# Moving two experts' up-products into the attention's last values, and what follows them one expert on

## The reference

```python
xn = layernorm(x)
s  = attn(xn)              # 16 heads of 8, window 128, softmax; + gated state-space branch; + MLP
g  = silu(ffn(xn))         # 8 experts, top 2, each 128 -> 2*128 -> 128
out = x + s * g

# in attn:
x1  = x + g*attn_out + (1-g)*ssm_out      # g = sigmoid(h @ Wg + bg)
h2  = layernorm(x1) * ln2_g + ln2_b       # the "second norm"
s   = x1 + gelu(h2 @ W1 + b1) @ W2 + b2
# in ffn, all experts for all rows, weighted by combine (0 where not chosen):
p1  = normed @ mlp1[e].T + bias           # "up-products": gate half and linear half
act = min(g, 7) * sigmoid(1.702*g) * (clip(lin, -7, 7) + 1)
out = xc + sum_e combine[e] * (act @ mlp2[e].T + bias)
```

## Time and profile before

| | us |
|---|---|
| runs of the kernel | 1091.38, 1097.93, 1089.91 |
| median | 1091.38 |
| profiled execution | 1094.57 |
| its span, first to last instruction | 1092.8 |
| mean granted TensorE clock | 0.925 of 2.4 GHz |

### The profile page before, as it was taken

One profiled execution on the slowest core, in us unless ns is written; L12 is line 12 of the kernel. 1 busy time (PEld: TensorE's weight loads), 2 busy tenths in 40 slices (PEclk: granted clock), 3 DMA queues, 4 the chain that ended last, 5 costly groups with the idle time before them and its releaser, 6 DMA issues.

```text
span 1092.8 us, 38402 instructions
## 1 busy us (share of the span) xinstructions
PE 919.2 (84%) x15864; PEld 561.7 (51%) x15864; DVE 782.5 (72%) x1990; ACT 712.8 (65%) x1126; POOL 501.8 (46%) x786
## 2 busy tenths in 40 slices
PE   2567898989889898988889898989888898978877
PEld 1333564646455464645555464645555464635435
DVE  4476777887877677888777777887777788656216
ACT  3205685858677595858768595867768585746645
POOL 6226355372736356273626456273635547152331
PEclk7557999999999899999999999998999999978869
DMA  5552414123332404224241503223241402310000
GB/s 108 129 118 67 93 46 105 32 94 64 100 62 75 90 27 108 50 90 62 92 75 53 112 24 109 52 90 63 75 93 36 111 17 99 58 31 6 25 1 10
DMA packets 85599, 75.24 MB, mean 69 GB/s; under 512 B 9329, under 2 KB 79154, under 8 KB 85426
## 3 DMA queue, kind: packets, MB, share of 16 engines
q1 hardware_dynamic: 83346, 72.00, 28.3%
q10 hardware_dynamic: 2080, 0.79, 0.3%
HBM read 36.33 MB, written 30.15 MB: 61 GB/s over the span
## 4 chain that ended last, share of the span: by engine, by line
PE 48%; DVE 25%; issue 13%; ACT 9%; POOL 2%; DMA 2%; DVEq 0%; SPq 0%; POOLq 0%; ACTq 0%
PE ps L558 8%; DVE mx L1074 6%; PE ps L500 6%; PE ps L690 5%; PE ps L750 5%; PE ps L711 5%; ACT pt L831 4%; PE ps L489 3%; DVE gc L1131 3%; PE ps L570 2%; DVE lin L1124 2%; PE ps L575 2%; ACT ot L836 2%; DVE junk L950 2%; PE ps L684 2%
## 5 line engine op out<-in xcount | busy, mean ns | idle before, releaser
L831 ACT ACTIVATE pt<-ps 128x1024 f32<-128x1024 f32 (+1 forms) x256 | 234.7, 917 | 212.5 <-PE ps L489 211.1
L1074 DVE TENSOR_REDUCE mx<-ps 128x2 f32<-128x320 f32 (+1 forms) x512 | 230.9, 466 | 110.6 <-PE ps L515 107.6
L1253 POOL TENSOR_SCALAR_AFFINE_SELECT pt<-pt 128x512 f32<-128x512 f32 x256 | 170.7, 669 | 264.6 <-ACT pt L831 264.3
L500 PE MATMUL ps<-kd,qz 48*32 48x160 bf16 (+1 forms) x4096 | 160.5, 241 | 66.6 <-DVE mx L1074 34.2
L489 PE MATMUL ps<-qz,kd 51*32 51x256 bf16 (+1 forms) x4096 | 183.5, 272 | 6.1 <-ACT pt L831 3.8
L558 PE MATMUL ps<-pt,va 128*32 128x256 f32 (+1 forms) x2048 | 159.8, 397 | 33.2 <-ACT ot L836 33.0
L500 PEld LDWEIGHTS ps<-kd,qz 48*32 48x32 bf16 x4096 | 72.7, 91 | 218.7 <-issue 121.3
L690 PEld LDWEIGHTS ps<-m,act_t 128*128 128x128 f32 x1024 | 126.8, 191 | 53.6 <-DVE act_t L1152 38.6
L690 PE MATMUL ps<-m,act_t 128*128 128x128 f32 x1024 | 143.2, 283 | 11.6 <-DVE act_t L1152 11.6
L1256 POOL TENSOR_SCALAR_AFFINE_SELECT pt<-pt 128x512 f32<-128x512 f32 x192 | 124.6, 649 | 0.0
L879 ACT ACTIVATE lin<-ps,mbias 128x512 f32<-128x512 f32 x128 | 87.7, 685 | 48.7 <-DVE act_t L1152 29.5
(11 more groups left out here) (158 smaller groups left out, 1672.7 us busy)
## 6 DMA issues: line engine op xcount, KB each, us to landing
qz<-qk_parts SPq DMA_DIRECT2D x32, 384.0 KB, 7.3
kd<-qk_parts SPq DMA_DIRECT2D x32, 384.0 KB, 8.7
qk_parts<-qp SPq DMA_DIRECT2D x16, 384.0 KB, 2.4
qk_parts<-kp SPq DMA_DIRECT2D x16, 384.0 KB, 2.3
xl<-L_attn_x SPq DMA_DIRECT2D x16, 256.0 KB, 3.1
qk_parts<-qp SPq DMA_DIRECT2D x16, 256.0 KB, 2.9
qk_parts<-kp SPq DMA_DIRECT2D x16, 256.0 KB, 2.7
xnr<-xn SPq DMA_DIRECT2D x16, 256.0 KB, 3.3
```

The source lines that it names most:

```text
L500: nc.tensor.matmul(ps[QG * c:QG * (c + 1), 4 + par, w * pr:w * (pr + 1)], qz[q][rows, 2 * g + pr, P * i + QG * c:P * i + QG * (c + 1)], kd ...
L831: nc.scalar.activation(to, src, ACT.Exp, scale=SCALE).then_inc(exp_ok.sem, 1)
L1074: nc.vector.tensor_reduce(mx[:, i, HG * g + pr:HG * (g + 1):2], src, AX.X, ALU.max).then_inc(mx_ok.sem, 1)
L1253: sel1 = nc.gpsimd.affine_select(out=pt[:, s, :, 0:P], in_=pt[:, s, :, 0:P], compare_op=ALU.is_ge, fill=0.0, base=0, pattern=[[0, HG], [1, ...
```

## The change

up(0) and the broadcast for expert 0 (now share(0), with a signal share_ps of its own) go behind values 13 (n = 16) on TensorE. up(1) and the transposes of nm go behind values 14 (n = 17). share(1) goes behind the transposes of ao, ahead of the product with wo, and waits for nmT, which leaves its bank 5. ScalarE no longer waits for the broadcast: up_ps stands for the two halves alone, and VectorE's gate waits for share_ps. ScalarE does lin(0) and ga(0) first and then aoT and nmT, ahead of lin(1). On VectorE both steps of the residual, the statistics of x1 and their moments come one expert later, and the first half of norm_stats comes behind expert 0 instead of 2. h2 goes from behind expert 4 to behind expert 5 (AT_H2), its transposes on TensorE from behind down(4) to behind share(7), ahead of down(5), and norm_x from behind expert 7 to behind expert 6, where it stands ahead of the copy to h2T.

```diff
-AT_H2 = 4
+AT_H2 = 5
...
+        share_ps = signal("share_ps", E)
...
+                def up(e):
+                    k = 3 * (e % 2)
+                    if e == 0:
+                        pe.wait_ge(*done(nfT_ok, b))
+                        pe.wait_ge(*done(exp_ok, b))
+                    elif e == 1:
+                        pe.wait_ge(*done(s1_ok, b))
+                        if nx2:
+                            pe.wait_ge(*done(gpre_ok, b + 2))
+                        if nxt:
+                            pe.wait_ge(*done(cT_ok, b + 1))
+                            pe.wait_ge(*done(mx_ok, b + 1))
+                    else:
+                        pe.wait_ge(*done(ga_ok, b, e - 1))
+                    for s in range(2):
+                        mm = nc.tensor.matmul(bank(k + s), m1[:, e, s], nfT[:, q], start=True, stop=True)
+                    mm.then_inc(up_ps.sem, 1)
+
+                def share(e):
+                    if e >= 2:
+                        pe.wait_ge(*done(gc_ok, b, e - 1))
+                    elif e == 1 and nxt:
+                        pe.wait_ge(*done(nmT_ok, b + 1))
+                    nc.tensor.matmul(bank(3 * (e % 2) + 2), sel[:, e], cT[:, q], start=True, stop=True).then_inc(share_ps.sem, 1)
...
+                    if main and n == NCH:
+                        up(0)
+                        share(0)
+                    if main and n == NCH + 1:
+                        up(1)
+                    if nxt and n == NCH + 1:
+                        turn_shift()
...
+                    share(1)
                     pe.wait_ge(*done(aoT_ok, b))
...
-                    up(1)
...
                     for e in range(2, E):
                         up(e)
+                        share(e)
+                        if e == 7:
+                            pe.wait_ge(*done(h2_ok, b))
+                            if nx2:
+                                pe.wait_ge(*done(lg_ok, b + 2))
+                            turn4(bank(6), lambda t: h2[:, t]).then_inc(h2T_ps.sem, 1)
...
                         down(e - 2)
-                        if e == 6:
-                            pe.wait_ge(*done(h2_ok, b))
-                            if nx2:
-                                pe.wait_ge(*done(lg_ok, b + 2))
-                            turn4(bank(6), lambda t: h2[:, t]).then_inc(h2T_ps.sem, 1)
...
-                if nxt:
+                def shift_out():
                     act.wait_ge(*done(nm_ps, b + 1))
                     act.wait_ge(*done(shift_in, b))
                     nc.scalar.activation(nmT[:], bank_bf(5)[0:NPART * H, :], ACT.Copy).then_inc(nmT_ok.sem, 1)
...
-                    act.wait_ge(*done(aoT_ps, b))
-                    act.wait_ge(*done(wo_ps, b - 1))
-                    nc.scalar.activation(aoT[:], bank(7), ACT.Copy).then_inc(aoT_ok.sem, 1)
...
+                        if e == 0:
+                            act.wait_ge(*done(aoT_ps, b))
+                            act.wait_ge(*done(wo_ps, b - 1))
+                            nc.scalar.activation(aoT[:], bank(7), ACT.Copy).then_inc(aoT_ok.sem, 1)
+                            if nxt:
+                                shift_out()
...
-                        if e == E - 1 and nx3:
+                        if e == 6 and nx3:
                             for t in range(NT):
                                 norm_x(t)
...
-
+                        dve.wait_ge(*done(share_ps, b, e + 1))
...
-                        if e == 0:
+                        if e == 1:
                             dve.wait_ge(*done(wo_ps, b))
...
-                        if e == 1:
+                        if e == 2:
                             dve.wait_ge(*done(x1_ok, b))
...
-                        if e == 0:
+                        if e == 1:
                             dve.wait_ge(*done(t1_ok, b))
...
-                        if e == 1:
+                        if e == 2:
                             dve.wait_ge(*done(st2_ok, b))
...
-                        if nx3 and e in (2, 3):
-                            norm_stats(b + 3, 1 - q, (0, 1) if e == 2 else (2, 3))
+                        if nx3 and e in (0, 3):
+                            norm_stats(b + 3, 1 - q, (0, 1) if e == 0 else (2, 3))
```

More of the change, by code:

```diff
@@ new lines, in share, with turn_shift @@
+                def share(e):
[4 more added lines that the diff above has]
+                    nc.tensor.matmul(bank(3 * (e % 2) + 2), sel[:, e], cT[:, q], start=True, stop=True).then_inc(share_ps.sem, 1)
+                def turn_shift():
+                    pe.wait_ge(*done(nm_step, b + 1))
+                    for t in range(NT):
+                        mm = nc.tensor.transpose(bank_bf(5)[0:NPART * H, P * t:P * (t + 1)], nm[:, t].rearrange("p r h -> p (r h)"), identb[:])
+                    mm.then_inc(nm_ps.sem, 1)
@@ new lines, in down, with turn_nf @@
+                def down(e):
+                    pe.wait_ge(*done(act_ok, b, e + 1))
+                    for t in range(NT):
+                        mm = nc.tensor.matmul(bank_t(7)[:, t], act_t[:, e % 3, P * t:P * (t + 1)], m2[:, e], start=False,
+                                              stop=e == E - 1, skip_group_check=True)
+                    mm.then_inc(down_ps.sem, 1)
+                def turn_nf():
+                    turn4(bank_bf(6), lambda t: nf[:, t]).then_inc(nfT_ps.sem, 1)
@@ new lines, in logits, with mlp_up @@
+                def logits():
+                    pe.wait_ge(*done(nfn_ok, b + 2))
+                    for t in range(NT):
+                        mm = nc.tensor.matmul(bank(6)[:, T // 2 + E * t:T // 2 + E * (t + 1)], nfn[:, P * t:P * (t + 1)], gw[:], start=True, stop=True)
+                    mm.then_inc(lg_ps.sem, 1)
+                def mlp_up(j):
+                    if j == 0:
+                        pe.wait_ge(*done(h2T_ok, b))
+                    elif j == 1:
+                        pe.wait_ge(*done(ga_ok, b, E - 1))
+                    elif j == 3:
+                        pe.wait_ge(*done(gc_ok, b, E - 1))
+                    nc.tensor.matmul(bank((6, 0, 1, 2)[j]), w1[:, P * j:P * (j + 1)], h2T[:], start=True, stop=True).then_inc(w1_ps.sem, 1)
@@ L667, in body @@
                     turn4(bank(7), lambda t: ao[:, t]).then_inc(aoT_ps.sem, 1)
-                def up(e):
-                    k = 3 * (e % 2)
-                    if e == 0:
-                        pe.wait_ge(*done(exp_ok, b))
-                    elif e == 1:
-                        pe.wait_ge(*done(s1_ok, b))
-                        if nx2:
[L676 to L711, removed]
@@ L713, in body @@
-                if main:
-                    pe.wait_ge(*done(nfT_ok, b))
-                    up(0)
+                    share(1)
                     pe.wait_ge(*done(aoT_ok, b))
@@ L859, in body @@
                     nc.scalar.activation(nmT[:], bank_bf(5)[0:NPART * H, :], ACT.Copy).then_inc(nmT_ok.sem, 1)
+                if nxt and not main:
+                    shift_out()
                 def nfn_in():
```

## The result

The changed kernel took 1143.79 us in the median of four runs (1133.33 to 1150.59), against 1093.97; the ratio is 1.042, 95% interval 1.033 to 1.052, which is 46 us. The ratios in this document leave out the runs of a slower state (here that of 1150.59 us), and what an edit gives back is reckoned from them. The forecast was 1115.0 us, at most 1127: the direction was right, the size was not. The profiled execution spans 1139.3 us, 46.5 more than before.

The account below looks back on a forecast made before the run. No engine bounds the whole; two dates decide, product 5's end on VectorE and h2T. 13 batches x 1.89 us = 24.6, less 1.0 for the last three, gave +23.6 us: 1115.0 us on the median, range 1102 to 1127.

Parts of the forecast that it names:

- the last three batches: Batches without norm_x in the loop: they keep the gain of about 0.3 us each, -1.0 us together.
- The hold of h2T: Tail: ScalarE waits for b1n and does norm_x before h2T, so mlp_up(0) starts 1.89 us late and TensorE stands 2.1 us.
- VectorE's stand at clip(1): Transition: aoT and nmT ahead of lin(1) on ScalarE make VectorE stand 0.88 us at clip(1).
- Moving h2 and the shift's DMAs: Tail and shift: h2 one expert later is free; the shift's DMA, some 3.9 us later, is covered by 5 us.
- The transition's term: Values 13 to 15: products and transposes between them take 1.30 us, ot comes 1.12 us late; product 5 still 0.32 early.
- rival (a): Clock falls in TensorE's new pause, mainly the tail: about 1.3 us per batch on 13 batches, 1132 us; chance 0.12.
- the sum's unchanged clock: Whole kernel: the sum of +23.6 us had no term for clock falls; most batches stayed at 1.00 in the trace.
- the prediction's own sign of being wrong: Changed trace: the forecast is wrong if the clock changes the period in most batches, instead of a steady period near 63.0 us.

Follow-up runs that it names:

- b_tail_busy_1: Kernel before, order unchanged, with 1.29 us of extra products on TensorE ahead of the first W1 product, batches 0 to 12: 1130.37 us, ratio 1.032.
- a_all_three_fills: Changed kernel with norm_x behind ga(7), the moved products behind values 15, five extra products ahead of values 4, 8 and 12: 1074.70 us, ratio 0.984.
- the shortest order: Changed kernel with norm_x behind ga(7), and up(0), share(0), up(1) and the transposes of nm behind values 15: 1088.22 us, ratio 0.997.

## Why the prediction was wrong

- **The count of the miss.** The forecast added 23.6 us, and the spans grew by 46.5. Of the missing 23, 8 are in the undisturbed batch (2.5 us instead of 1.89, over 13 batches), 16 are stretches at 1.2 GHz and pauses, for which the sum had nothing, 2 are in the start-up, and the last three batches gave back 2.5 more.
- **The hold of h2T** was right in mechanism and size: the pause 2.05 us (2.1), aoT to h2T 15.45 us (15.7), h2T to the next scores 9.80 (9.89). Undone it gave back more than itself, 29 us by the ratios against 22.
- **VectorE's stand at clip(1)** was right: 0.77 us (0.88), put down to lin(1). Moving h2 and the shift's DMAs was free, as said: the second hop was issued at 198.81, 4.15 us behind the first, 20 us ahead of its reader.
- **The transition's term was mis-sized.** I let ot come 1.12 us late; it came 1.72 late. The step was "0.43 + 0.21 + 0.43, and 0.23 for the transposes, in all 1.30 us": array time alone. The rows show no weight load for 0.41 to 0.42 us at four changes, between values (tiles of 128 by 32), products (128 by 128) and the transposes of nm (128 by 48). Values 13 hold TensorE 0.57 us, up(0) with share(0) 0.76, where I had 0.43 and 0.64. The Trainium skill, "TensorEngine Tiling (Array Packing)", Key Properties, says that a change of tiling mode drains TensorE. The trace agrees: 0.1 us or more is lost at each change, and that rule, which speaks against this change, should have been in the sum. With everything else as forecast it makes the way from the last Exp to the next batch's first 2.5 us longer; 2.0 was measured, since h2T and the rest came sooner than I had it. That this is near the forecast's 1.89 is luck: two errors of 0.6 and 0.5 us met.
- **A term that was not in the sum:** 0.5 us behind the first Exps of each batch. The second and third distances between them are 1.94 and 2.16 us instead of 1.77 and 1.82. There one step of VectorE's finish falls together with GpSimd's second mask, and takes 1.02 us instead of 0.68. In the batches that the table counts, each kernel with the tail late (norm_x early, or b_tail_busy_1) has the 1.02, and each with norm_x behind ga(7) and no longer tail has 0.68. So it comes with the late tail; that the mask is the cause was not tried. The rows, before and after:

```profile
587.70 0.68 DVE L926 SCALAR_TENSOR_TENSOR sres<-zth,sres 128x512 f32<-128x512 f32 x1
587.71 1.16 POOL L1253 TENSOR_SCALAR_AFFINE_SELECT pt<-pt 128x512 f32<-128x512 f32 x1 [0.32 <-ACT pt L831]
...
222.37 1.02 DVE L944 SCALAR_TENSOR_TENSOR sres<-zth,sres 128x512 f32<-128x512 f32 x1
222.81 1.08 POOL L1274 TENSOR_SCALAR_AFFINE_SELECT pt<-pt 128x512 f32<-128x512 f32 x1
```

- **The step that failed is the chance of rival (a)**, and with it the sum's unchanged clock. "TensorE also had pauses of about 1 us without a fall in most steady batches", and so 0.12. I took the kernel's 5 falls as a constant of the kernel and looked only for new pauses. The row that warned was mine: a batch at 0.95 took 3.5 us more; and the prediction's own sign of being wrong, a clock that changes the period in most batches, is what came. What I had not asked is what a longer batch does to the old thin places. A longer batch without a new pause (b_tail_busy_1) lost some 15 us beyond its own length; filling the new pause with norm_x early changed nothing; filling the old place ahead of values 12 moved the falls away from it. But rival (a) as I wrote it is not refuted: of the executions whose stages are read, none without the tail's pause has a stretch behind that place (at 53 to 58 us) in batches 0 to 12, and four of the five with the pause do, 2 of 13 in the changed kernel, 6 of 13 with the products behind values 15, 6 of 9 and 3 of 3 with the chunks filled. In the changed kernel that is 2 x 1.7 = 3.4 of the 16 us. The Trainium skill, "TensorE: Matmul & The Clock Gate", Part 1, says that the share of the clock's pulses that is passed is set by how busy the array has been recently; with the thin chunks filled the clock stays at 2.4 GHz (a_all_three_fills, no stretch in batches 0 to 12), which agrees.
- **The last three batches** gained 3.5 us in all instead of 1.0; which part of that is the clock, no run tells.
- **What stays open:** why 5 falls become 13 to 19 when a batch gets longer. The count is no plain rule of the length: with norm_x back a batch is 61.6 us, with both edits undone 60.4, and both have 9, with a batch of 62.4 us b_tail_busy_1 has 19. That series of batches repeat at 64.8 to 64.9 us with the fall at the same place, in kernels of different undisturbed length, suggests that the fall and the length hold each other; it was not shown, and executions of one kernel differ by up to 20 us.

## What to carry to other kernels

Ask of each step that is moved in an engine's order what it waits for and who stands behind it: norm_x was 1.64 us of ScalarE in spare time, and ahead of h2T it held TensorE for 2.05 us. Work put between the values on TensorE costs its array time and the changes of tile shape around it; behind values 15 the same products cost 1.16 us less per batch. And where the clock falls in some batches, 1 us more in a batch may cost nearly 3 (35 us over 13 batches, from 1.02 us of products): look for the thin places first, and try to fill them; here five products whose result nobody reads brought 14 us in the shortest order, 5 in the changed kernel, within the noise, and nothing in the kernel before.

## What the hardware showed unexpectedly

A busy TensorE made faster kernels: with 15 extra products per batch the granted clock is 1.00 in every batch window shown and the kernel is 1.6% faster than the one before, but only together with the order edits undone; five extra products alone in the kernel before brought nothing (0.996 to 1.002).

TensorE sometimes issues nothing for over a microsecond in the midst of a chunk, at full clock and with nothing in the profile that it waits for; so in the batch of 219.57 us of the changed kernel:

```profile
238.69 0.09 PEld L490 LDWEIGHTS ps<-qz,kd 51*32 51x32 bf16 x1
240.04 0.10 PEld L490 LDWEIGHTS ps<-qz,kd 51*32 51x32 bf16 x3 [1.26 <-issue]
```

The Exp behind it came 3.27 us after the one ahead of it instead of 1.95. Batches 3 and 4 of the kernel before show the same at the same chunk, 3.29 and 3.17 us. It is part of what I summed as disturbance, about 1 us in such a batch.
